# A's products of five units spread one by one between the products of x and W, with small moves on four engines

## The reference

```python
# r_x [2048, 1024], r_user_indices, r_item_indices [2048], W_base [1024, 1024], A [16, 1024]
# B_user, B_item [1250, 1024, 16], W_common [1024, 16]; SCALING = 2
base = x @ W_base.T + b_base
a = x @ A.T
Bu = B_user[user_indices]
Bi = B_item[item_indices]
user_part = jnp.einsum('bor,br->bo', Bu, a)
item_part = jnp.einsum('bor,br->bo', Bi, a)
common_part = a @ W_common.T
return base + SCALING * (user_part + item_part + common_part)
```

## Time and profile before

| | |
|---|---|
| median of three runs | 222.88 us |
| the profiled execution: its time, its span | 223.5 us, 221.7 us |
| TensorE (PE) busy, of the span | 213.9 us, 96% |
| its weight loads (PEld) | 172.8 us, 78% |
| VectorE (DVE) | 169.1 us, 76% |
| GpSimd (POOL) | 70.0 us, 32% |
| ScalarE (ACT) | 55.3 us, 25% |
| granted TensorE clock, mean | 0.999 of full |

### The profile page before, as it was taken

One profiled execution on the slowest core, in us unless ns is written; L12 is line 12 of the kernel. 1 busy time (PEld: TensorE's weight loads), 2 busy tenths in 40 slices (PEclk: granted clock), 3 DMA queues, 4 the chain that ended last, 5 costly groups with the idle time before them and its releaser, 6 DMA issues.

```text
span 221.7 us, 3023 instructions
## 1 busy us (share of the span) xinstructions
PE 213.9 (96%) x1122; PEld 172.8 (78%) x1122; DVE 169.1 (76%) x261; ACT 55.3 (25%) x87; POOL 70.0 (32%) x81
## 2 busy tenths in 40 slices
PE   7999999799999997999999999999999999989995
PEld 7777887587777875877887788878887888868894
DVE  1889988899499799999999999399997982070411
ACT  3686526434011120034100223045010600000000
POOL 6010250040324422415643263114544240573000
PEclk9999999999999999999999999999999999999999
DMA  6999999755739975798899999866899948158121
GB/s 203 394 415 370 268 338 412 259 206 233 228 94 312 385 279 234 218 286 330 318 282 308 362 281 313 312 256 235 296 333 367 356 174 190 42 171 159 56 100 49
DMA packets 14816, 57.76 MB, mean 261 GB/s; under 512 B 3828, under 2 KB 4468, under 8 KB 10812
## 3 DMA queue, kind: packets, MB, share of 16 engines
q0 software_dynamic: 7344, 35.30, 47.5%
q1 hardware_dynamic: 7168, 21.73, 27.6%
q10 hardware_dynamic: 288, 0.52, 0.7%
HBM read 58.95 MB, written 11.01 MB: 316 GB/s over the span
## 4 chain that ended last, share of the span: by engine, by line
PE 50%; DVE 21%; DMA 18%; SPq 5%; issue 3%; ACT 2%; DVEq 0%; POOLq 0%
PE main_ps L1012 14%; PE main_ps L1014 14%; PE main_ps L1013 14%; DVE acc L731 11%; DMA rows<-table,fetch 7%; DMA out_sb<-table 6%; DVE x_lo L634 4%; DMA set_sums<-acc 2%; PE main_ps L1078 2%; SPq L295 2%; DMA x_hi_raw<-set_sums,back 2%; DVE a_turned L684 2%; SPq L298 1%; PE ps_b L968 1%; PE ps_b L969 1%
## 5 line engine op out<-in xcount | busy, mean ns | idle before, releaser
L731 DVE SCALAR_TENSOR_TENSOR acc<-rows,a_entry,acc 128x1024 f32<-128x1024 f32 x75 | 96.3, 1284 | 8.6 <-DMA rows<-table,fetch 6.5
L1012 PE MATMUL main_ps<-w_hi,x_hi 128*128 128x512 f32 (+1 forms) x224 | 87.9, 392 | 0.0
L1014 PE MATMUL main_ps<-w_hi,x_lo 128*128 128x512 f32 (+1 forms) x224 | 86.5, 386 | 0.0
L1013 PE MATMUL main_ps<-w_lo,x_hi 128*128 128x512 f32 (+1 forms) x224 | 86.5, 386 | 0.0
L399 POOL DMA_INDIRECT rows<-table,fetch x40 | 50.4, 1261 | 105.5 <-DVE acc L731 92.9
L1014 PEld LDWEIGHTS main_ps<-w_hi,x_lo 128*128 128x128 f32 x224 | 42.1, 188 | 8.7
L1012 PEld LDWEIGHTS main_ps<-w_hi,x_hi 128*128 128x128 f32 x224 | 42.1, 188 | 7.9
L1013 PEld LDWEIGHTS main_ps<-w_lo,x_hi 128*128 128x128 f32 x224 | 42.2, 188 | 7.8
L634 DVE TENSOR_TENSOR x_lo<-x_lo_raw,x_hi 128x1024 fp32r<-128x1024 f32 (+2 forms) x19 | 19.9, 1054 | 1.3 <-ACT x_hi L483 1.0
L523 ACT ACTIVATE out_sb<-main_ps 128x1024 f32<-128x1024 f32 x12 | 12.2, 1018 | 31.8 <-PE main_ps L1014 30.5
L483 ACT ACTIVATE x_hi<-x_lo_raw 128x1024 fp32r<-128x1024 f32 (+2 forms) x18 | 16.8, 946 | 10.7 <-DMA x_lo_raw<-x_t 10.7
(11 more groups left out here) (116 smaller groups left out, 158.6 us busy)
## 6 DMA issues: line engine op xcount, KB each, us to landing
out<-out_sb SPq DMA_DIRECT2D x15, 512.0 KB, 6.0
x_lo_raw<-x_t SPq DMA_DIRECT2D x14, 512.0 KB, 8.2
w_lo_raw<-w_t SPq DMA_DIRECT2D x7, 512.0 KB, 7.2
x_lo_raw<-x_t SPq DMA_DIRECT2D x3, 256.0 KB, 5.5
rows<-table,fetch POOLq DMA_INDIRECT x40, 8.1
w_lo_raw<-w_t ACTq DMA_DIRECT2D x2, 256.0 KB, 4.2
set_sums<-acc SPq DMA_DIRECT2D x1, 512.0 KB, 5.1
out_sb<-table SPq DMA_DIRECT2D x6, 64.0 KB, 12.4
```

Source lines behind the costliest of these rows:

```text
L731: return dve.scalar_tensor_tensor(to, rows_r, a_r, to, ALU.mult, ALU.add)
L1012: pe.matmul(to, x_hi[:, u % RING, k, x], w_hi[:, k, o], start=start, stop=False)
L1013: pe.matmul(to, x_hi[:, u % RING, k, x], w_lo[:, k, o], start=False, stop=False)
L1014: return pe.matmul(to, x_lo[:, u % RING, k, x], w_hi[:, k, o], start=False, stop=stop)
```

## The change

- The 16 products of A for units 3 to 7 are no longer one block. `base_and_a` does three `k` of a tile's base products, 18, and puts one product of A behind each of the first 16. The first `k` of the stretch is the one that stood just ahead of the block, in all five units: k = 4 for unit 3, k = 2 for unit 4, k = 3 for units 5 to 7.
- TensorE: `pack_entries(1)` stands two `k` earlier, ahead of `turn_low(3)`.
- VectorE: the turning of unit 2 stands ahead of both pieces of `x_lo` of unit 3, and the second piece behind `take_rows(1)`. The second piece of `x_lo` of unit 5 stands one chunk of row products earlier, and `take_entries(2)` one chunk earlier.
- GpSimd: the add of set 2 stands behind `bring_back` instead of ahead of it.
- The last tile is done in two halves. The second half is one sum of 512 columns and one VectorE instruction; it is stored in two quarters, one issued by SyncE and one by ScalarE.
- At the start, the first half of `w_hi` at k = 0 is made in two quarters, by ScalarE and by VectorE.

```diff
-            make_first_w_hi(0, w_half_loaded)
-            make_first_w_hi(1, w_loaded[0])
+            make_first_w_hi(slice(0, QUARTER), w_half_loaded)
+            make_first_w_hi(half_of(1), w_loaded[0])
...
+            dve.wait_ge(w_half_loaded, 16)
+            dve.tensor_copy(w_hi[:, 0, QUARTER:BANK], w_raw[:, 0, QUARTER:BANK]).then_inc(w_first_hi, 1)
             make_x_lo(0, 0)
+            dve.wait_ge(w_first_hi, 1)
...
             gather(4, range(0, CHUNKS))
+            bring_back()
             add_to_out(2)
-            bring_back()
             add_to_out(3)
...
+            t, o = TILES - 1, slice(BANK + QUARTER, OUT_F)
+            act.wait_ge(evacuated, t + HALVES)
+            act.dma_start(out[t * P:(t + 1) * P, o], out_sb[:, t % 2, o]).then_inc(stored[t % 2], 16)
...
             spread_values(1)
+            turn_a_values(2)
             make_x_lo(3, 0)
+            spread_values(2)
+            take_rows(1)
             make_x_lo(3, 1)
-            take_a(2)
-            take_rows(1)
             take_entries(0)
...
             make_x_lo(5, 0)
-            row_products(1, range(2, 3))
             make_x_lo(5, 1)
-            row_products(1, range(3, 5))
+            row_products(1, range(2, 5))
             make_onehot(3)
             take_a(5)
-            row_products(1, range(5, CHUNKS))
+            row_products(1, range(5, 7))
             take_entries(2)
+            row_products(1, range(7, CHUNKS))
...
+                for term in range(TERMS):
+                    x_part, w_part = (x_lo if term == 2 else x_hi), (w_lo if term == 1 else w_hi)
+                    done = pe.matmul(to, x_part[:, u % RING, k, x], w_part[:, k, o], start=start and term == 0,
+                                     stop=stop and term == TERMS - 1)
+                    if a_from is not None and a_from + term < A_PRODUCTS:
+                        a_product(a_of, a_from + term)
...
-            base(2, range(4, 5))
-            rank_a(3)
-            base(2, range(5, KC), stop=False)
+            base_and_a(2, range(4, 7), 3)
+            base(2, range(7, KC), stop=False)
...
             base(3, range(0, 2))
+            pack_entries(1)
             turn_low(3)
-            base(3, range(2, 4))
-            pack_entries(1)
-            base(3, range(4, KC)).then_inc(tile_done, 1)
+            base(3, range(2, KC)).then_inc(tile_done, 1)
...
-                    base(t0, range(1, 3))
-                    rank_a(4)
-                    base(t0, range(3, KC)).then_inc(tile_done, 1)
+                    base(t0, range(1, 2))
+                    base_and_a(t0, range(2, 5), 4)
+                    base(t0, range(5, KC)).then_inc(tile_done, 1)
```

More of the change, by code:

```diff
@@ L52 @@
 MAINS = 3
+A_PRODUCTS = 2 * KC
+TERMS = 3
 BLOCKS = 8
@@ L88, in brought_of, with half_of @@
     return [j for j, (of, tab) in enumerate(BACK) if of == t]
-def parts_of(n):
-    last = n == TILES - 1
-    return ((0, BANK), (BANK, 3 * BANK // 2), (3 * BANK // 2, OUT_F)) if last else ((0, BANK), (BANK, OUT_F))
+def half_of(part):
+    return slice(part * BANK, (part + 1) * BANK)
+QUARTER = BANK // 2
 def piece_of(u, h):
@@ L1022, in base, with base_and_a @@
                 for k in ks:
-                    for part in range(len(parts_of(t))) if parts is None else parts:
+                    for part in parts:
                         done = base_step(t, part, k, start and k == 0, stop and k == KC - 1)
                 return done
+            def base_and_a(t, ks, a_of):
+                a_from = 0
+                for k in ks:
+                    for part in range(HALVES):
+                        base_step(t, part, k, a_of=a_of, a_from=a_from)
+                        a_from += TERMS
             def first_tiles(k):
@@ L1039, in first_tiles @@
                         pe.wait_ge(w_hi_done, k + half + 1 if k == 0 else k + 2)
+                    if k == 0 and half == 0:
+                        pe.wait_ge(w_first_hi, 1)
                     for t in range(UT):
```

86 lines of the change are left out of this document (40 added, 46 removed).

## The result

The changed kernel takes 221.38 us (median of five runs; the kernel before 222.91 beside it). The ratio is 0.9924, with a 95% interval of 0.9897 to 0.9951: faster, by 1.5 us between the medians, under 1% of the time. The ratio is one of means and leaves out one of the five runs, 224.74 us, which was in a slower state with a mean clock of 0.990; by it the gain is 1.7 us. The forecast was 3.8 us less (219.1), and its range ended at 221.3. So the sign was right and the size was not: less than half of the gain came.

A forecast was written before the change was run, and what follows sets the result against it. TensorE, 96% busy, bounds the kernel, VectorE's sums arriving almost together at 195. 0.67 + 3.43 = 4.10 us less at left_of(7), 0.13 more at the end, 0.2 given back: 3.8 less, 219.1 us; range 218.4 to 221.3.

The forecast's parts named there:

- The four waits: TensorE at pack_rows(1), A of unit 5, pack_rows(3), left_of(7): 1.58, 1.73, 0.47 and 0.67 us, all expected to go.
- Rival 3: Weight loads show at the 80 base products behind A's; 0.08 us each, 6.6 us, kernel slower at 225.7 us; chance 0.06.
- rival 1: The sums' line stays late: set_sums write still takes 5.12 us, left_of(7) at 193.02, kernel 220.8 us; chance 0.15.
- rival 4: Waits at 40.6 and 87.2 return elsewhere for as long and the write keeps its time; 222.8 us; chance 0.05.
- a sign of 0.13 us behind A's products: Sign of being wrong: base products follow A's products by more than 0.13 us.
- one of a microsecond: Sign of being wrong: TensorE waits a microsecond or more at units 4 to 6 for ps_b.
- I take 0: TensorE, 80 products of A between base products: no stall, cost 0; bounds 0.5 us more, 0.1 us less.
- VectorE's 2.27 us: VectorE from take_entries(1) on: 2.72 us of wait go, less 0.45 us for unit 3's later turning, 2.27 us earlier throughout.
- rival 2: VectorE gains less than 2.27 us because unit 3's turning comes later; 220.4 us, or 221.4 with no gain; chance 0.14.
- the last tile: End of kernel: products 0.29 us less, VectorE 0.27 more, last store 0.15 more; sum 0.13 us more.
- the 0.2 that I gave back: Taken off the 3.97 us gain for three places with slack under 0.5 us, leaving 3.8 us.
- the median of the runs lies 0.6 us below it: Last step: from the profiled execution's forecast, 219.7 us, to the runs' median, 219.1 us.

The follow-up runs named there:

- e1: Changed kernel with A's products of units 3 to 7 again as blocks of 16 at their old places; 220.07 us, ratio 0.9861.
- e9: Changed kernel with A's products of units 3 to 7 over only the first 128 of 256 columns; one run, 221.03 us.
- e13: Changed kernel storing only the first 64 of tile 3's 1024 columns, 480 KB less under way between 64 and 75 us; one run, 220.2 us.
- e3: Changed kernel with the old tail: last tile in three sums, last 128 KB stored by SyncE alone; 220.89 us, ratio 0.9891.
- e5: Changed kernel with A's products in blocks and the last half tile stored by SyncE in one 256 KB transfer; 219.91 us, ratio 0.9852.
- e12: Kernel before with only the add of set 2 moved behind the transfers back; 222.94 us, ratio 0.9985.
- e7: Kernel before with the moves and the first w_hi; no interleaving, new tail or later add; 219.01 us, ratio 0.9808.
- e6: Changed kernel with A's products in blocks and the old three-sum tail, last 128 KB stored alone; 219.59 us, ratio 0.9832.
- e11: Kernel before with two moves: turning of unit 2 ahead of unit 3's x_lo pieces, pack_entries(1) ahead of unit 3's turning; 221.30 us, ratio 0.9909.
- e10: e6 with the first half of w_hi made by ScalarE in one piece, as before the change; 219.42 us, ratio 0.9821.
- e4: Kernel before with only A's products of units 3 to 7 put one by one between base products; 225.79 us, ratio 1.01.
- e16: e6 run once more unchanged, with its profile, to see why its runs spread; one run, 220.67 us.

## Why the prediction was right in sign and wrong in size

**What held.** The four waits went. Without interleaving left_of(7) would come at 190.83 by my terms (195.28 - 0.67 - 3.78), and e1 measured 190.36. take_entries(1) came 2.12 us earlier (2.27 forecast), the turning of unit 3 at 48.63 (48.36). The write of set_sums took 2.6 us. The start gave nothing. Rival 3's cost was real, at a tenth of its price; rival 1 did not happen, and of rival 4 a part did, 1.4 us of waits in other places. (Rival 3's 80 x 0.08 is 6.4 us and not 6.6, and its time 225.5 us; nothing hangs on it.) Most of the signs that I had named for being right came and those for being wrong did not, since a sign of 0.13 us behind A's products can't show a cost of 0.0075 us each, and one of a microsecond can't show four waits of 0.2 to 0.7.

**The step that failed first: "I take 0" for the interleaving.** It cost 0.6 us of cadence. I had two rows for it: one base product on time behind A's block, and 47 intervals of 0.120 us where each load of 128 weight columns stands behind 256 columns. The second is the repeated pattern, and it was the right one: 0.006 us there, 0.0075 us measured for a pair, 0.6 us in all. I kept it as a bound only. The Trainium skill's rule that I quoted ("TensorE: Matmul & The Clock Gate", section "LDWEIGHTS (loading the stationary operand)"), 107 ns for 128 weight columns, agrees with the 0.11 us between the turnings' products and nearly with the 0.112 us of e9. It does not fit the packs' bf16 products, 0.03 us apart with as many weight columns; there the measurement decides. What makes the 0.0075 us of a pair at 256 columns stays open.

**The second: VectorE's 2.27 us as constant from take_entries(1) on.** "Its later waits are for gathers, which are issued as it sets slots free, and so move with it." The issues moved, the landings did not: 1 us was lost at 72 to 76 us, and e13 shows that the bytes under way there did it. Another 0.8 us went behind 155 us (1.53 us ahead at take_entries(4), 0.69 at the writing), which is within what that stretch varies between two runs of one kernel. Everything that I had set against it was off by that: the bank at unit 6 waited 0.72 us instead of 0.15, x_lo of unit 5 ended at 83.35 instead of 82.31 (0.24 us of wait instead of a slack of 0.4), the turning ahead of it 0.20 instead of 0 (and 0.25 before the change, which I hadn't seen). This is rival 2 in kind, from another cause than the one that I gave it.

**The third: the last tile,** +0.13 forecast, +0.7 measured (27.2 against 26.4 us; e3 gives 0.5 by medians, 0.8 by spans). The products were worth a little more than 0.29 us and VectorE cost 0.27 as put; the store cost 2.5 - 1.7 = 0.8 us instead of 0.15. I had let two stores run side by side at the price of one of their size. One store of 256 KB would have been no better (2.38 us in e5), so the term was the 256 KB at the end, and not the two engines.

**The sum again:** at left_of(7) the missing 1.36 us are 0.6 of cadence, 0.57 + 0.24 + 0.06 + 0.20 of waits, 0.09 of start, less 0.4 by which the removed waits were worth more than 3.78 (0.25 of it is the wait at the turning ahead of unit 5). At the end 0.6 of tail is added, and the 0.2 that I gave back is used up. That explains the profiled execution, 221.34 us where 219.7 were forecast, to 0.1 us.

**The fourth: "the median of the runs lies 0.6 us below it".** I took 0.6 us off because the profiled execution of the kernel before (223.5) lay that far above its median. After the change the profiled execution and the median are the same (221.34, 221.38), so these 0.6 us are missing too, over a quarter of the 2.3 us by which 219.1 was off. A likely reason is the wait of 0.67 us at left_of(7): without it the span before would be 221.0 us, and over half of the 52 runs of the kernel before have 220.7 to 221.3; and e12, whose profile has no such wait, can't be told from the kernel before. Then the usual run had little of this wait to lose, and the 0.67 us of the sum were a gain in the profiled run alone. There is only one profile of the kernel before, so this isn't shown.

**What the change consists of, then:** the moves alone gave some 4.3 us (e7, ratio 0.9808, first w_hi included). From there one step at a time leads to the changed kernel, by the medians: the add behind the transfers 219.01 to 219.59 (e6), the interleaving to 220.89 (e3), the new tail to 221.38. Of these steps the interleaving is the large one, 1.3 us, and 2.2 us at left_of(7) in e1; the other two lie within the intervals. That e11, with two of the moves, equals the whole is a coincidence of sizes: what the other moves gave, the interleaving, its earlier demand and the tail took back. The best versions are e7 (219.01), e10 (219.42) and e6 (219.59 us), 1.7 to 1.9% below the kernel before and about 1% below the changed one; their intervals overlap, and none of the three is shown to be the best.

Open: the 0.0075 us of a pair, the 2.38 us of 256 KB at the very end against 2.0 shortly before, and which traffic makes the gathers at 157 to 180 us late in some runs.

## What to carry to other kernels

When work is spread out to fill gaps, price the spreading as a thing of its own: what the new neighbours cost each other, by the row that repeats most and not by the one that is cheapest, and what asks sooner or ends later because of it. Ask of every lead that is carried forward whether the transfers behind it can move too; here, at a DMA share of 0.95, they did not, and half of the lead was gone at once. Look for waits from start to start, before as well as after. And don't carry the distance between one profiled execution and the median over to the changed kernel. And where two lines arrive within a microsecond of each other, shortening one hands the end, and its run-to-run spread, to the other.

## What the runs showed of the hardware

- Between f32 products with 128 weight columns a product of 128 columns costs 0.112 to 0.119 us, nearly as much as one of 256 (0.120 to 0.125), though 128 columns are worth 0.057; the shortfall appears behind the longer product, not ahead of it (e9: 0.06 us ahead, 0.28 to 0.29 behind instead of 0.228). Six bf16 products of 6 columns, 128 weight columns each, take 0.17 us together, and 0.08 more behind the next base product.
- A TensorE wait of 2.15 us (bracket) was followed by some 3 us at 1.2 GHz, which cost 1.6 us more (e4, one trace; seven of its eight runs have the same mean clock). Waits up to 1.74 us (e16, and the kernel before) were not, in the runs profiled.
- A wait of up to 0.26 us behind a product of 512 columns carries no bracket, since it hides under that product's modelled end. Three of them cost 0.7 us here.
- A 512 KB write took 2.6 us with the adds behind it (thirteen profiles) and 3.7 to 5.15 us beside a read-and-write of the same size (five).
